# Products for attention's maxima from quarters of the array, around the weighted values

## What is computed

```python
qkv = jnp.einsum('bsi,oi->bso', x, w_qkv) + b_qkv          # b=4, s=1024, 256 -> 3*256
qkv = qkv.reshape(b, s, HEADS, 3 * HEAD_DIM).transpose(0, 2, 1, 3)   # 16 heads of 16
q, k, v = jnp.split(qkv, 3, axis=-1)
attn = jnp.einsum('bhqd,bhkd->bhqk', q, k) * scale
attn = jax.nn.softmax(attn, axis=-1)
vals = jnp.einsum('bhqk,bhkd->bhqd', attn, v)
out = jnp.einsum('bse,oe->bso', vals.reshape(b, s, EMBED), w_o) + b_o
...
x = x + ga * attention(layernorm(x) * (1 + ca) + sa)
x = x + gb * experts(layernorm(x) * (1 + cb) + sb)         # 32 experts, top 6, and a shared one
```

## Time and profile before

| what | value |
|---|---|
| median of 3 runs | 1425.0 us (1424.52 to 1428.65) |
| the profiled execution, its own time | 1430.49 us |
| its span | 1428.7 us, granted clock 0.975 on average |
| PE busy | 1359.2 us, 95% |
| DVE busy | 1129.7 us, 79% |
| ACT busy | 754.5 us, 53% |
| POOL busy | 606.7 us, 42% |

### The profile page before, as it was taken

The page is one execution under the profiler, slowest core; times in us unless marked ns, Lnnn a source line. Parts: engine busy times, 40 slices in busy tenths (PEclk is TensorE's granted clock), DMA queues, the critical chain, the costliest instruction groups (busy, mean ns, idle before and its releaser), DMA issues.

```text
span 1428.7 us, 30863 instructions
## 1 busy us (share of the span) xinstructions
PE 1359.2 (95%) x8207; PEld 677.6 (47%) x8208; DVE 1129.7 (79%) x2815; ACT 754.5 (53%) x1155; POOL 606.7 (42%) x782
## 2 busy tenths in 40 slices
PE   7997999999999999999999999989999999999996
PEld 3552223332333323333333233558788888887552
DVE  7886999999999999999999992656566666665477
ACT  3772577667666767676667677113333333333100
POOL 4000113233744725546346366327755555555200
PEclk9997799999999999999999999999999999999998
DMA  6887355534346435454465346837766656555788
GB/s 213 273 266 201 102 165 134 112 91 106 99 127 166 103 101 140 124 135 101 112 162 146 80 134 198 257 124 237 226 202 203 203 168 189 180 173 173 270 304 317
DMA packets 216960, 243.55 MB, mean 170 GB/s; under 512 B 93949, under 2 KB 181501, under 8 KB 216738
## 3 DMA queue, kind: packets, MB, share of 16 engines
q1 hardware_dynamic: 189330, 166.42, 42.8%
q0 software_dynamic: 21776, 68.07, 13.4%
q10 hardware_dynamic: 5760, 7.87, 1.7%
HBM read 133.98 MB, written 108.28 MB: 170 GB/s over the span
## 4 chain that ended last, share of the span: by engine, by line
PE 68%; DVE 14%; DMA 5%; issue 2%; SPq 1%; ACT 1%; POOL 0%; DVEq 0%; POOLq 0%
PE psO L1171 14%; PE ex_psGU L1670 13%; PE psE L1158 13%; PE psM L1148 9%; DVE piece_max L1046 9%; PE ex_psY L1685 6%; PE ex_psX L1661 3%; PE psM L505 2%; PE co_psS L1935 2%; PE ex_psA L1679 2%; DMA wide<-results 1%; DMA results<-vals_inv,places 1%; PE psGU L1486 1%; PE late_psGU L1915 1%; PE psM L524 1%
## 5 line engine op out<-in xcount | busy, mean ns | idle before, releaser
L1046 DVE TENSOR_REDUCE piece_max<-psM 128x1 f32<-128x512 f32 x1024 | 642.2, 681 | 28.6 <-PE psM L1148 25.3
L1112 ACT ACTIVATE wide<-psE 128x1024 f32<-128x1024 f32 x512 | 497.1, 1021 | 208.4 <-PE psE L1158 206.2
L1148 PE MATMUL psM<-wide 48*128 48x512 bf16 x1024 | 324.5, 396 | 20.4 <-DVE piece_max L1046 12.0
L1158 PE MATMUL psE<-wide 49*128 49x512 bf16 (+1 forms) x2048 | 331.0, 382 | 2.4 <-DMA wide<-maxima 2.4
L1752 POOL DMA_INDIRECT results<-vals_inv,places x223 | 213.9, 959 | 155.9 <-DVE vals_inv L1738 89.9
L1171 PE MATMUL psO<-wide 128*32 128x512 f32 x2048 | 275.4, 610 | 0.6 <-ACT wide L1112 0.6
L1148 PEld LDWEIGHTS psM<-wide 48*128 48x128 bf16 x1024 | 78.2, 93 | 348.4 <-DVE piece_max L1046 275.8
L1670 PE MATMUL ex_psGU<-wide,ex_xT 128*128 x892 | 233.0, 384 | 0.6 <-ACT ex_xT L1703 0.6
L1158 PEld LDWEIGHTS psE<-wide 49*128 49x128 bf16 (+1 forms) x2048 | 117.9, 95 | 94.0 <-issue 10.4
L1670 PEld LDWEIGHTS ex_psGU<-wide,ex_xT 128*128 128x128 f32 x892 | 153.1, 192 | 15.6 <-issue 2.9
L1703 ACT ACTIVATE ex_xT<-ex_psX 128x256 f32<-128x256 f32 x223 | 85.6, 384 | 123.7 <-PE ex_psX L1661 122.5
(11 more groups left out here) (280 smaller groups left out, 1271.8 us busy)
## 6 DMA issues: line engine op xcount, KB each, us to landing
wide<-qk_parts SPq DMA_DIRECT2D x384, 64.0 KB
wide<-results SPq DMA_DIRECT2D x16, 1536.0 KB, 8.6
rows<-lists SPq DMA_DIRECT2D x112, 160.0 KB
h2Ts<-lists SPq DMA_DIRECT2D x111, 160.0 KB
qk_parts<-parts SPq DMA_DIRECT2D x32, 384.0 KB, 3.0
xin<-in_x_dram SPq DMA_DIRECT2D x16, 512.0 KB, 4.0
v_values<-vst SPq DMA_DIRECT2D x32, 256.0 KB, 3.6
wide<-v_values SPq DMA_DIRECT2D x16, 512.0 KB
```

The costliest lines, as they stand in the source:

```text
L1046: v.tensor_reduce(piece_max[:, qh, (x * PAIRS + h) * KT // QH + qt, kh:kh + 1], bank_of("piece", PIECES * group + n), AX.X, ALU.max, negat ...
L1112: nc.scalar.activation(probs[:, step % 2, 2 * pair:2 * pair + 2], psE[:, pair], ACT.Exp, scale=HD ** -0.5).then_inc(exp_ok, 1)
L1148: nc.tensor.matmul(bank_of(*user), qa[g][rows, h, qt * P:(qt + 1) * P], ka[g][rows, h, kh * 512:(kh + 1) * 512], start=True, stop=True).th ...
L1158: mm = nc.tensor.matmul(psE[:, pair, x], k[g][part, pair, kt * P:(kt + 1) * P], q[g][part, pair, qh * 512:(qh + 1) * 512], start=(q is qa) ...
```

## The change

Pieces leave out one of the three products (MID HI), so that they need 32 rows (`QUARTER`) instead of 48; the maximum is then that of a rounded product, which serves to keep the exponentials in range as before. In the half of a head pair, head h=0 has its two products for pieces in rows 0 to 31 and the third behind, head h=1 has them in rows 32 to 63, the third in rows 16 to 31 and zeros in rows 0 to 15 (`LEAD_AT`, `LAST_AT`). So the pieces of both heads of both halves lie in four different quarters, and the order of pieces has h as its fastest index: a and b are the two heads of x=0, c and d those of x=1. The scores of pair 1 take 64 rows of `qa` instead of 49.

Since the heads now lie in different partitions, the load of `qa` and `ka` takes one transfer per head (24 of 32 KB), that of `qb` and `kb` one per pair as before (12 of 64 KB). `SHARE` becomes 8. The row of the maxima moves to `qb`, and the ones to `kb`; POOL also writes the zeros.

In a step PE now does all eight scores, pieces a and b, the weighted values, pieces c and d, and what it hosts.

```diff
+QUARTER = 2 * HD
+LEAD_AT = (0, QUARTER)
+LAST_AT = (QUARTER, HD)
...
-LOADS = 2 * 2 * 2 * TERMS + 1
+LOADS = 2 * 2 * 3 * TERMS + 1
...
             for x in range(2):
-                for to, part in zip(rows, parts):
-                    at = HALF * x + HD * r
-                    of = ((g % 2) * HG + x * (HG // 2)) * HD
+                of = ((g % 2) * HG + x * (HG // 2)) * HD
+                for h in range(HG // 2):
+                    at = HALF * x + (LEAD_AT[h] + HD * r if r < TERMS - 1 else LAST_AT[h])
                     if first <= n < end:
-                        sp.dma_start(
-                            to[g][at:at + HD],
-                            env.qk_parts[q_or_k, part[r], b, g // 2, of:of + HG // 2 * HD, :]
-                            .rearrange("(h d) t -> d h t", d=HD)).then_inc(env.loaded[g], 16)
+                        sp.dma_start(lead[g][at:at + HD, h],
+                                     env.qk_parts[q_or_k, lead_part[r], b, g // 2, of + h * HD:of + (h + 1) * HD, :]
+                                     ).then_inc(env.loaded[g], 16)
                     n += 1
+                at = HALF * x + HD * r
+                if first <= n < end:
+                    sp.dma_start(small[g][at:at + HD],
+                                 env.qk_parts[q_or_k, small_part[r], b, g // 2, of:of + HG // 2 * HD, :]
+                                 .rearrange("(h d) t -> d h t", d=HD)).then_inc(env.loaded[g], 16)
+                n += 1
...
-    SHARE = 5
+    SHARE = 8
...
-                    wait(pool, env.key_ones, 2 * h + x)
-                    g.memset(env.ka[h][at:at + HALF // 2], 1.0).then_inc(env.key_ones, 1)
+                    g.memset(env.kb[h][at:at + HALF // 2], 1.0).then_inc(env.key_ones, 1)
+                    for to in (env.qa, env.ka):
+                        g.memset(to[h][HALF * x:HALF * x + QUARTER, 1], 0.0).then_inc(env.key_ones, 1)
...
+            n, h = divmod(n, PAIRS)
             n, x = divmod(n, 2)
             n, kh = divmod(n, 2)
-            n, qt = divmod(n, KT // QH)
-            qh, h = divmod(n, PAIRS)
+            qh, qt = divmod(n, KT // QH)
...
-                    sp.dma_start(qa[g][at:at + 1, :, qh * S // QH:(qh + 1) * S // QH],
+                    sp.dma_start(qb[g][at:at + 1, :, qh * S // QH:(qh + 1) * S // QH],
...
-                rows = slice(HALF * x, HALF * x + QROWS)
+                rows = slice(HALF * x + LEAD_AT[h], HALF * x + LEAD_AT[h] + QUARTER)
...
-                scores(step, g, s, 0)
+                wait(pe, exp_ok, 2 * (step - 1) + 1)
+                for x in range(2):
+                    score(g, s, 0, x, False)
+                for x in range(2):
+                    last = score(g, s, 0, x, True)
+                last.then_inc(scored, 1)
+                wait(pe, exp_ok, 2 * (step - 1) + 2)
+                score(g, s, 1, 0, False)
+                score(g, s, 1, 1, False)
+                score(g, s, 1, 0, True)
+                score(g, s, 1, 1, True).then_inc(scored, 1)
                 if to < NGR:
                     piece(to, first)
-                scores(step, g, s, 1)
-                if to < NGR:
                     piece(to, first + 1)
```

More of the change, by code:

```diff
@@ L132, in load_group @@
     for r in range(TERMS):
-        for q_or_k, (rows, parts) in enumerate((((env.qa, env.qb), Q_PART), ((env.ka, env.kb), K_PART))):
+        for q_or_k, (lead, small, (lead_part, small_part)) in enumerate(
+                ((env.qa, env.qb, Q_PART), (env.ka, env.kb, K_PART))):
             for x in range(2):
-                for to, part in zip(rows, parts):
-                    at = HALF * x + HD * r
-                    of = ((g % 2) * HG + x * (HG // 2)) * HD
+                of = ((g % 2) * HG + x * (HG // 2)) * HD
+                for h in range(HG // 2):
+                    at = HALF * x + (LEAD_AT[h] + HD * r if r < TERMS - 1 else LAST_AT[h])
                     if first <= n < end:
-                        sp.dma_start(
-                            to[g][at:at + HD],
-                            env.qk_parts[q_or_k, part[r], b, g // 2, of:of + HG // 2 * HD, :]
-                            .rearrange("(h d) t -> d h t", d=HD)).then_inc(env.loaded[g], 16)
+                        sp.dma_start(lead[g][at:at + HD, h],
+                                     env.qk_parts[q_or_k, lead_part[r], b, g // 2, of + h * HD:of + (h + 1) * HD, :]
+                                     ).then_inc(env.loaded[g], 16)
                     n += 1
+                at = HALF * x + HD * r
[4 more added lines that the diff above has]
+                n += 1
     if first <= n < end:
@@ L224, in fetch_queries_keys @@
                 if c == CPB:
-                    sp.wait_ge(env.key_ones, 2 * NG)
+                    sp.wait_ge(env.key_ones, 6 * NG)
                     for j in range(QKT):
@@ L1150, in piece, with score @@
                                  ).then_inc(piece_done, 1)
-            def scores(step, g, s, pair):
-                wait(pe, exp_ok, 2 * (step - 1) + pair + 1)
+            def score(g, s, pair, x, small):
                 qh, kt = s // KT, s % KT
[L1155 to L1159, removed]
-                                              stop=(q is qb))
-                mm.then_inc(scored, 1)
+                q, k, rows = (qb, kb, QROWS + 1) if small else (qa, ka, HALF if pair else QROWS)
+                part = slice(HALF * x, HALF * x + rows)
+                return nc.tensor.matmul(psE[:, pair, x], k[g][part, pair, kt * P:(kt + 1) * P],
+                                        q[g][part, pair, qh * 512:(qh + 1) * 512], start=not small, stop=small)
             def weighted_values(step):
```

## The result

| | kernel before | changed kernel |
|---|---|---|
| median | 1426.8 us (4 runs, 1424.5 to 1434.3) | 1482.4 us (4 runs, 1481.2 to 1491.4) |
| ratio | | 1.039, 95% interval 1.034 to 1.045 |
| span of the profiled execution | 1428.7 us | 1481.7 us |
| first weighted values start | 157.2 us | 169.6 us |
| from there to those of the last step | 727.8 us | 769.4 us |

The forecast was 1452 us, range 1431 to 1467: slower, as it said, but by twice as much. Of the 53.0 us of span, 12.4 lie ahead of attention's first weighted values and 41.6 between them and those of the last step; 1.0 comes back behind them.

A forecast was written before the change was run, and what follows sets the result against it. Taken to bound it: a 2.49 us loop per step of c, its reduction on DVE, b in c's bank and the weighted values. 20 + 2 + 1 + 4 = 27 us on the 1425.0 us median gave 1452, range 1431 to 1467.

The forecast's parts named there:

- The passages on PE: Two more switches per step between halves and quarters, 0.10 us each; over 160 steps +20.0 us.
- POOL's memsets: Zeros and ones written at the start take 14.4 us more, but nothing waits for them: 0.
- SP's lateness: In attention, loads 6.1 us longer make the exchanges of maxima late: +4 us.
- The order: All eight scores before a and b: columns on PE's path neither gained nor lost, apart from passages.
- the step of 2.61: In attention, a plain step on PE from c to the next c takes 2.61 us instead of 2.49.
- the hosted steps: Steps in which PE also does hosted products: only the passage before a is new, +2 us.
- Pairs side by side: On PE, a and b run together in their quarters, as do c and d.
- the third rival: On PE, pairs in quarters don't overlap, b starting 0.22 us after a: about 1530 us; chance 0.08.
- The first rival: Half to quarter costs nothing on PE and SP alone decides, maxima 11 us late: 1436 us; chance 0.20.
- the second: Rival: no passage cost on PE, c and d run beside scores: 1422 us, or 1408; chance 0.12.
- SP in the projections: Three more transfers per chunk cost 1.5 us, a store goes 0.8 us late, others wait for DVE anyway: 0.

The follow-up runs named there:

- e7: Changed kernel with the even exchange of maxima put behind 20 of a load's 37 transfers, the other 17 after it: 1488.5 us, ratio 1.0447.
- e12: Kernel before with ones written over all 128 partitions in 4-byte elements and the even exchange put behind 19 of a load's 25 transfers: 1426.7 us, ratio 1.0006.
- e14: Kernel of e9 with pieces in whole halves and group 3's last 8 transfers behind the load of group 0's sums: 1436.3 us, ratio 1.0058.
- e9: Changed kernel with 4-byte memsets over all 128 partitions and the last 8 of a load's 37 transfers behind the even exchange: 1465.5 us, ratio 1.0298.
- e5: The changed kernel run again as it is, for comparison on another chip: 1478.1 us, ratio 1.0403 to the kernel before.

## Why the prediction was wrong

The passages on PE were forecast rightly. What failed are two terms beside PE: POOL's memsets, put at 0, cost 7 us, and SP's lateness, put at 4 us by its idle alone, cost some 13, because half clock follows the idle. The order and small waits, put at nothing, are the rest.

By medians: the changed kernel again took 1478.1 us, with both side costs mended 1458.1, with halves 1436.3, and the kernel before 1426.6 beside each of them. So 20.0 us are side costs on SP and POOL, 21.9 are quarters, 9.7 what is left of order, loads and waits. Short memsets alone brought 7.1 of the 20.0. None of these is known better than to some 5 us: the four executions of the changed kernel again lie between 1476.2 and 1495.7.

- **Passages: right, in mechanism and size.** 0.10 us each, in both directions; the step of 2.61 is what was forecast to the hundredth. Forecast 23 us with the hosted steps, measured 21.9 by medians and some 21 from the steps' usual lengths. What the Trainium skill, TensorEngine Tiling (Array Packing), Tiling Modes, Key Properties, says of draining fits this trace. That going between 64 and 32 rows is such a change is shown by 2.61 us against 2.49, and the price of 0.10 comes from the runs alone.
- **Pairs side by side: right.** The weighted values come 0.32 us after a and b, the columns of one and a passage, so the third rival falls. The first rival (no price) and the second fall with the step.
- **POOL: wrong, 0 for 7 us.** The step was "done near 31 us; the first load that waits for them stands in the projections' third chunk: 0". I followed who waits for the memsets by a semaphore and not who works beside them. The memsets alone, on the kernel before, cost 0.54%; short memsets bring attention 10 us forward, and the time by 7. The kernel before showed it: such an operation of DVE on four numbers, in its line summary:

```profile
L110 DVE TENSOR_SCALAR mean<-mean x4: 169/170/1529, 11.2 to 47.7; 128x4 f32<-128x4 f32 x4
```

  170 ns, and 1529 while POOL writes. The Trainium skill, SBUF — State Buffer, Who interferes with whom, states that DVE in some of its modes shares a pair of ports with GpSimd, that the instruction that comes first holds it to its end, and that the other blocks. The trace agrees: the first TENSOR_SCALAR on L125 of the changed kernel ends at 14.68 us, 0.03 after the memset beside it. Operations on two tensors in SBUF (L111 of the changed kernel, 157 to 159 ns) don't slow down beside the memsets, as that page has it for a GpSimd operation that doesn't read.
- **SP in attention: mechanism right, term too small.** A load takes 5.8 us more (18.6 for 37 transfers), against 6.1 forecast, and the first late exchange adds 1.8 us of idle (3.05 less 1.25), against 1.7. Over all it is 5.7 us (8.1 less 2.4) against 4. The step that failed priced the wait by its idle alone. Where PE sits 3 us the clock falls, and the two steps of the first late exchange take 9.9 us in place of 6.3 before. With the next one, 10.5 for 5.0 (it waits 2.56 us, where 1.0 was forecast), two exchanges cost 9 us, of which 0.5 is the longer plain step. The 13 us over all is the 20.0 of both side costs less the 7.1 of the memsets; no run took SP's part away alone, since e7 moved it to another wait.
- **SP in the projections: about right.** The loads alone left the start where it was. With short memsets, the stores of queries and keys take 90.9 us from first to last (26.8 to 117.6), and 89.6 before the change (28.2 to 117.8), so 1.3 where I had 0; but e12, with the loads of before, has 90.5, so most of that needn't be the loads.
- **The order: not quite nothing.** 0.13 to 0.20 us more in four of each 32 steps, all with hosted products or right behind them (e14 beside the kernel before), so 4 to 5 us in all; 1.0047 alone. The other 5 of the 9.7 us I can't divide.
- **The start's clock.** It was no term of the sum. Some 6 us of the first trace are its late rise, which the second trace doesn't have at the same median, so this explains the trace and not the result. Whether quarters make it more likely is open.

What stays open is why the clock falls in some executions and not in others; single executions of the same kernel scatter by up to 20 us with it (1456.9 to 1471.8 in e9, 1476.2 to 1495.7 in e5). It doesn't fall just anywhere. Behind attention's opening, each stretch at 1.2 GHz in the traces from e5 on, the changed kernel and the kernel before either comes with a wait of PE of 1.4 to 4.1 us (an exchange or a division that is late) or begins in step 22, 23 or 27 of a window of 32, that is in one of the last two steps with hosted products or right behind one. The windows view of one of the latter, kernel before, with short waits of PE for banks in the first row:

```profile
785.00:788.00 3.00, 2.27 (x12) 0.43 (x11) 3.00 (x8) 1.48 (x2) 0.00 (x0) 1.00 0.00 0
788.00:791.00 3.00, 2.68 (x18) 1.04 (x18) 2.92 (x10) 1.02 (x1) 1.88 (x7) 0.54 0.00 0
791.00:794.00 3.00, 3.00 (x16) 0.64 (x16) 1.33 (x3) 1.02 (x1) 0.79 (x3) 0.50 0.05 9
```

Most such stretches last 3.4 or 6.8 us. The same steps of other windows and other executions keep 2.4 GHz, and no run was made to take these stretches away.

## What to carry to other kernels

Put down every tile shape in the order in which PE takes them, and count the passages: each costs 0.10 us here, so neighbours of one shape belong together and a gain in rows must buy its passages. A memset by GpSimd isn't free while VectorE works: operations that scale one tensor in SBUF (TENSOR_SCALAR) were held by it here, those on two tensors and the reciprocal (178 ns in every trace) were not. A late transfer costs its idle and can cost steps at half clock with it: in these traces (from e5 on, the changed kernel and the kernel before) each of the 13 waits of PE of 1.98 to 4.10 us in attention has a stretch of 1.2 GHz beside it, and 3 of the 12 waits of 1.07 to 1.66 us. Mending one place in a queue that works in order can make the next one late, so look for where the queue is idle.

## What the runs showed that was not expected

A step in mixed shapes has no overlap between them: with six passages the sum of columns and passages gives the 3.03 us to the hundredth. A memset of 512 4-byte elements takes 0.53 us over 128 partitions and 0.53 to 0.55 over 32, so filling all partitions, most of which the loads overwrite, took POOL 8.0 us where the changed kernel took 30.1. An exchange of 4 KB through memory takes 5.9 us from the first store to the scores when nothing is late (231.57 to 237.44 in the kernel before), though its six transfers keep SP for 2.8.
